# Graph attention on one core: P turned by VectorE in 32x32 blocks and moved through DRAM, K and V projected in bursts, values three tiles behind

## The reference

```
q, k, v = (x @ Wq), (x @ Wk), (x @ Wv)      each reshaped to (8, 2048, 256)
a = q @ k.T / 16 + adj + adj                # per head, 2048 x 2048
a = where(adj == 0, -1e6, a);  a = softmax(a);  a = where(adj == 0, 0, a)
out = layernorm(x + concat_heads(a @ v) @ Wout)
```

## Time and profile before

| | |
|---|---|
| median of three runs | 2095.36 us |
| span of the profiled execution, first to last instruction | 2092.3 us |
| time around that span, against the median of the runs | 3.1 us |
| TensorE busy | 2043.2 us, 98% |
| VectorE busy | 1159.7 us, 55% |
| ScalarE busy | 843.0 us, 40% |
| GpSimd busy | 264.9 us, 13% |
| DMA | 226.42 MB, mean 108 GB/s |

### The profile page before, as it was taken

One profiled execution on the slowest core, in us unless ns is written; L12 is line 12 of the kernel. 1 busy time (PEld: TensorE's weight loads), 2 busy tenths in 40 slices (PEclk: granted clock), 3 DMA queues, 4 the chain that ended last, 5 costly groups with the idle time before them and its releaser, 6 DMA issues.

```text
span 2092.3 us, 36481 instructions
## 1 busy us (share of the span) xinstructions
PE 2043.2 (98%) x12320; PEld 1789.0 (86%) x12320; DVE 1159.7 (55%) x2852; ACT 843.0 (40%) x1364; POOL 264.9 (13%) x207
## 2 busy tenths in 40 slices
PE   7899999999999999999999999999999999999997
PEld 7777788888888888888888888888888888888886
DVE  7788874454545445454555454455445445445555
ACT  4333333443443444334434434443344343343333
POOL 5111111101101101111011011011011111000000
PEclk9999999999999999999999999999999999999999
DMA  6766643333333333233333333333333332323332
GB/s 234 234 205 202 205 141 102 88 89 100 86 101 96 85 96 95 82 101 85 90 103 88 96 94 86 98 99 85 95 100 86 97 96 80 99 81 83 83 87 74
DMA packets 145607, 226.42 MB, mean 108 GB/s; under 512 B 12928, under 2 KB 70272, under 8 KB 143488
## 3 DMA queue, kind: packets, MB, share of 16 engines
q1 hardware_dynamic: 145536, 225.50, 36.9%
HBM read 206.57 MB, written 18.87 MB: 108 GB/s over the span
## 4 chain that ended last, share of the span: by engine, by line
PE 87%; DVE 5%; DMA 2%; issue 2%; ACT 0%; DVEq 0%; SPq 0%
PE bank L153 31%; PE bank L677 19%; PE bank L146 14%; PE bank L676 10%; PE bank L661 10%; DMA m_dram<-m_build 2%; DVE m_build L255 2%; PE bank L673 1%; PE bank L674 1%; DVE t_p L221 1%; DVE zero_mark L243 1%; DVE pt_l L209 0%; DVE k L209 0%; DVE y_acc L519 0%; DVE y_acc L914 0%
## 5 line engine op out<-in xcount | busy, mean ns | idle before, releaser
L153 PE MATMUL bank<-k,q_split 128*128 128x512 f32 x3072 | 840.8, 409 | 3.5 <-DVE k L209 2.5
L677 PE MATMUL bank<-v,pt_h 128*128 128x512 f32 x1856 | 673.5, 395 | 0.0
L153 PEld LDWEIGHTS bank<-k,q_split 128*128 128x128 f32 x3072 | 541.5, 190 | 95.7 <-issue 4.4
L209 DVE TENSOR_TENSOR pt_l<-bank,pt_h 128x512 fp32r<-128x512 f32 x496 | 342.7, 691 | 401.5 <-PE bank L153 392.5
L171 ACT ACTIVATE pt_h<-bank 128x512 fp32r<-128x512 f32 x496 | 296.2, 597 | 615.3 <-PE bank L661 615.2
L676 PE MATMUL bank<-v,pt_l 128*128 128x256 f32 x1856 | 522.5, 282 | 0.0
L677 PEld LDWEIGHTS bank<-v,pt_h 128*128 128x128 f32 x1856 | 348.9, 188 | 69.2
L676 PEld LDWEIGHTS bank<-v,pt_l 128*128 128x128 f32 x1856 | 350.5, 189 | 13.6
L221 DVE CUSTOM_DVE_ANT_0 t_p<-bank,m_sb 128x512 f32<-128x512 f32 x512 | 348.2, 680 | 1.8 <-PE bank L153 1.8
L176 ACT ACTIVATE t_p<-t_p,small 128x2048 f32<-128x2048 f32 x128 | 256.4, 2003 | 164.7 <-DVE small L229 157.5
L661 PE MATMUL bank<-ident,t_p 128*128 128x128 f32 x2048 | 307.6, 273 | 5.8 <-ACT t_p L176 3.7
(11 more groups left out here) (69 smaller groups left out, 1394.7 us busy)
## 6 DMA issues: line engine op xcount, KB each, us to landing
m_sb<-m_dram SPq DMA_DIRECT2D x508, 256.0 KB, 3.2
adj_chunk<-in_adj_dram SPq DMA_DIRECT2D x64, 256.0 KB, 3.0
raw_w_q<-in_L_gnn_Wq_dram SPq DMA_DIRECT2D x63, 256.0 KB, 3.7
raw_w_k<-in_L_gnn_Wk_dram SPq DMA_DIRECT2D x56, 256.0 KB, 3.9
raw_w_v<-in_L_gnn_Wv_dram SPq DMA_DIRECT2D x56, 256.0 KB, 4.1
m_dram<-m_build SPq DMA_DIRECT2D x14, 1024.0 KB, 5.0
raw_x<-in_x_dram SPq DMA_DIRECT2D x8, 256.0 KB, 4.4
place<-in_L_gnn_Wv_dram SPq DMA_DIRECT2D x8, 256.0 KB, 6.4
```

The source lines that it names most:

```text
L153: mm = nc.tensor.matmul(score_bank[b][:], q_split[:, a, k, f * P:(f + 1) * P], k_both[:, kk, k, b * BANK:(b + 1) * BANK], start=(i == 0), ...
L209: ins = nc.vector.tensor_tensor(dst, src, hi.bitcast(F32), ALU.subtract)
L677: mm = nc.tensor.matmul(*hi_v, start=False, stop=(g == BANKS - 1 and j == TPB - 1))
```

## The change

**P's path.** The transposes on TensorE are gone. VectorE turns `t_p` (all 2048 columns, one instruction) in blocks of 32x32 into `blocks`, sorted by the block's place inside its 128 columns (`turn`). SP stores `blocks` to DRAM (`park`, 1 MB, rows of 8 KB), and loads it back in four pieces of 256 KB (`shuffle`), piece i from 32 rows of DRAM to all 128 partitions, so that each 128x128 block lies fully turned in `p_turned`. ScalarE writes the high part (`hi_p`), GpSimd the low part (`lo_p`), each in four pieces a tile. The values of a tile are multiplied three steps after its scores (`LAG = 3`), and P's split and the sum in PSUM have two buffers.

**K and V.** There is one K and one V buffer. All eight K slices of a head are projected in one burst ahead of its tile 0, all eight slices of V (transposed and times Wout) in one burst ahead of tile 3's scores. Weights go through five slots, loaded five ahead. Every projection and every bank of scores takes the next of a ring of six PSUM banks; two more hold the sums. Q stays one slice per two tiles.

**M.** It is loaded whole (1 MB), by ScalarE's queue, into one of two buffers. In head 0 one tile of M is made during the tile before, with two `adj_chunk` buffers, whose loads stand between the loads of P in SP's order. The prologue is gone, and all code is unrolled.

```diff
+LAG = 3
+RING = 6
+SLOTS = 5
+        p_dram = nc.dram_tensor("p_dram", [2, P, N], F32, kind="Internal").ap()
+        m_sb = [sbuf(f"m_sb{i}", [P, N]) for i in range(2)]
+        blocks = [sbuf(f"blocks{i}", [P, N]) for i in range(2)]
+        p_turned = sbuf("p_turned", [P, N])
+        p_split = [sbuf(f"p_split{i}", [P, 2, N], F32R) for i in range(2)]
+        adj_chunk = [y_acc[:, Y_LATE + 2 * i:Y_LATE + 2 * i + 2, :].rearrange("p a d -> p (a d)") for i in range(2)]
...
+                def park(tau):
+                    sp.wait_ge(turned, tau + 1)
+                    if tau >= 2:
+                        for i in range(QUADS):
+                            sp.wait_ge(shuffled[i], 16 * (tau - 1))
+                    sp.dma_start(p_dram[tau % 2], blocks[tau % 2][:]).then_inc(parked, 16)
+
+                def shuffle(tau, i):
+                    if i == 0:
+                        sp.wait_ge(parked, 16 * (tau + 1))
+                    if tau:
+                        sp.wait_ge(p_lo, 4 * (tau - 1) + i + 1)
+                    sp.dma_start(p_turned[:, i * BANK:(i + 1) * BANK],
+                                 p_dram[tau % 2][quad(i), :].rearrange("p (j b) -> j p b", j=QUADS)
+                                 ).then_inc(shuffled[i], 16)
...
+                for tau in range(ALL + 1):
+                    h, t = divmod(tau, TILES)
+                    if h == 0:
+                        store_m(t)
...
+                    if opens:
+                        if h:
+                            load_wout(h)
+                        load_w_behind("k", h, 2)
+                    if sums:
+                        load_w_behind("vt", h, 1)
+                    if tau:
+                        park(tau - 1)
+                    for i in range(QUADS):
+                        if opens:
+                            load_w_behind("k", h, 3 + i)
+                        if sums:
+                            load_w_behind("vt", h, 2 + i)
+                        if tau:
+                            shuffle(tau - 1, i)
+                        if h == 0 and t + 1 < TILES:
+                            load_adj((t + 1) * BANKS + i)
...
+                for tau in range(ALL + LAG):
+                    h, t = divmod(tau, TILES)
+                    if tau < ALL and t == 0:
+                        if h:
+                            wait_emptied(("x", h))
+                        for c in range(C):
+                            project_x(("k", h, c))
+                        project_x(("q", h, 0))
+                    if tau < ALL and t == VALUES_FROM:
+                        pe.wait_ge(wout_lo, h + 1)
+                        for c in range(C + 1):
+                            if c < C:
+                                project_x(("vt", h, c))
+                            if c:
+                                wait_emptied(("vt", h, c - 1))
+                                project(("v", h, c - 1), vt_split[(c - 1) % 2], w_out)
+                    for g in range(BANKS):
+                        if tau < ALL:
+                            scores(tau, g)
+                            if g == 1 and t % 2 == 0 and t <= LAST_Q:
+                                project_x(("q", h, t // 2 + 1))
+                            if g == 1 and t == TURN_X and h + 1 < H:
+                                turn_x(h + 1)
+                        if tau >= LAG:
+                            values(tau - LAG, g)
...
+                def hi_p(tau, i):
+                    if i == 0 and tau >= 2:
+                        act.wait_ge(y_done, tau - 1)
+                    act.wait_ge(shuffled[i], 16 * (tau + 1))
+                    nc.scalar.activation(by_chunk(p_split[tau % 2][:, HI])[:, :, i, :],
+                                         p_turned[:, i * BANK:(i + 1) * BANK].rearrange("p (j b) -> p j b", b=QUAD),
+                                         ACT.Copy).then_inc(p_hi, 1)
...
+                def turn(tau):
+                    if tau >= 2:
+                        dve.wait_ge(parked, 16 * (tau - 1))
+                    dve.wait_ge(exp_done, tau + 1)
+                    nc.vector.transpose(blocks[tau % 2][:].rearrange("p (q j b) -> p j q b", q=QUADS, b=QUAD),
+                                        t_p[:].rearrange("p (j q b) -> p j q b", q=QUADS, b=QUAD)
+                                        ).then_inc(turned, 1)
```

More of the change, by code:

```diff
@@ L80, in graph_attention_layernorm @@
-        before = ExitStack()
[L81 to L85, removed]
+        k_split = sbuf("k_split", [P, 2, KC, N], F32R)
+        v_split = sbuf("v_split", [P, CHUNKS, 2, D], F32R)
+        q_split = [sbuf(f"q_split{i}", [P, 2, KC, R], F32R) for i in range(2)]
+        vt_split = [sbuf(f"vt_split{i}", [P, 2, KC, R], F32R) for i in range(2)]
@@ L122, in graph_attention_layernorm @@
[L122 to L128, removed]
+        ln = sbuf("ln", [P, 144])
@@ L140, in graph_attention_layernorm @@
         TERMS = [(a, b, k) for k in range(KC) for a, b in ((HI, HI), (HI, LO), (LO, HI))]
[L142 to L186, removed]
@@ new lines, in _, with store_out @@
+                assert loaded[0] == len(w_keys)
+                def store_out(first, stop):
+                    for f in range(HALVES):
+                        sp.dma_start(out_tokens[f][:, first:stop], y_tokens[:, f, first:stop]).then_inc(stored, 16)
+                sp.wait_ge(normed, 8)
+                store_out(0, 4)
+                sp.wait_ge(normed, TILES - 2)
+                store_out(4, C - 1)
+                for f in range(HALVES):
+                    sp.wait_ge(normed, TILES - 1 + f)
+                    sp.dma_start(out_tokens[f][:, C - 1], y_tokens[:, f, C - 1]).then_inc(stored, 16)
@@ new lines, in score @@
+                def score(tau, b):
+                    r, t = home["s", tau, b][0], tau % TILES
+                    dve.wait_ge(scores_done, BANKS * tau + b + 1)
+                    if b == 0 and tau >= TILES:
+                        dve.wait_ge(m_loaded[tau % 2], 16 * (tau // 2 - TILES // 2 + 1))
+                    if b == 0 and tau:
+                        dve.wait_ge(turned, tau)
+                    if tau < TILES:
+                        dve.wait_ge(m_chunk, (tau + 1) * BANKS)
+                    nc.vector.tensor_tensor_reduce(out=t_p[:, b * BANK:(b + 1) * BANK], in0=bank[r][:],
+                                                   in1=m_sb[tau % 2][:, b * BANK:(b + 1) * BANK], scale=2.0,
+                                                   scalar=LOWEST, op0=ALU.add, op1=ALU.max,
+                                                   accum_out=maxima[:, t, b:b + 1]).then_inc(emptied[r], 1)
@@ new lines, in denominator @@
+                def denominator(tau):
+                    t = tau % TILES
+                    dve.wait_ge(floor_done, tau + 1)
+                    nc.vector.scalar_tensor_tensor(out=row_sum[:, t:t + 1], in0=floor_exp[:, t:t + 1],
+                                                   scalar=count[:, t:t + 1], in1=row_sum[:, t:t + 1],
+                                                   op0=ALU.mult, op1=ALU.add).then_inc(denom_ready, 1)
+                    dve.wait_ge(denom_ready, tau + 1)
+                    nc.vector.reciprocal(rdenom[:, t:t + 1], row_sum[:, t:t + 1]).then_inc(rdenom_ready, 1)
```

1047 lines of the change are left out of this document (445 added, 602 removed).

## The result

The changed kernel takes 2813.19 us (median of 4 runs, 2807.79 to 2815.39) against 2095.32 us before: a ratio of 1.3429, 95% interval 1.341 to 1.3448. It is 34% slower. The forecast was 2560 us, slower, range 2180 to 2830.

The account below looks back on a forecast made before the run. TensorE, busy 2043.2 of 2092.3 us, was taken to bound the kernel before. Forecast: 7 heads x (16 x 18.2 + 10) = 2109, head 0 400, 27 before the first store, 25 after the last: 2560 us, range 2180 to 2830.

Parts of the forecast that it names:

- The mechanism: Loads of P in every tile: source counts 4 outermost, so four DMA engines carry each, 2.73 us a load.
- The period: Per tile on those four engines: 18.2 us taken, low 16.8, high 19.4; above 16.0 slower than before.
- 10.9, 2.4 and 2.6 us: Parts of one period: P's four loads 10.9 us, the store's share 2.4, one fixed latency 2.6.
- M's and the weights' 3.5: End of each period: M's share 2.4 us and weights 1.1, which may fall into the 2.6 us latency or not.
- its stock of three tiles keeps the DMA engines fed, all but 0 to 10 us a burst: Two bursts a head: TensorE stalls, its stock keeps DMA fed; 0 to 20 us lost a head, 10 taken.
- Head 0: Ring of store, loads of P and adj, last chunk, add_y, transpose: 25.3 us, less with overlap; 16 x 25 = 400 us.
- Start and end: Before the first store 27 us (K burst 13, first load and splits 8, scores and exponential 6); after the last 25.
- The forecast's own high sum: Whole kernel, upper end: 7 x (16 x 19.4 + 20) + 450 + 60 = 2823 us.
- Costs on the engines: Per tile: VectorE 8.4 us with transpose 2.4, ScalarE 7.3 to 9.7, GpSimd 7.2 to 12.4, all beside TensorE's 14.4.
- rival D: VectorE's 32x32 transpose or GpSimd's strided low parts take several times longer and set the period: 2110 us or more; chance 0.04.
- Rival C: TensorE, waiting each tile, gets half clock half the time, its 14.4 us become 21.6: 2874 us; chance 0.05.
- Rival B: The four loads run on all 16 engines, TensorE's 14.4 us a tile rule: 2038 us, faster; chance 0.14.

Follow-up runs that it names:

- 16-engine version: Against the changed kernel, P stored so each load's source is 128 contiguous rows, the store in four transfers: 2159.52 us, ratio to before 1.0313.

## Why the prediction was right, and what it mis-sized

**The mechanism: right.** Four engines carry the loads of P (4 small packets each, and one row of padding switches between 2160 and 2917 us); their period sets the pace of the regular steps; TensorE waits at values for `p_lo`, 293.6 us in 70 waits. A load was taken at 2.73 us on four engines and came 2.5 to 2.6 us behind the one before it, once 3.2. By the rule of the Trainium skill ("DMA: Bandwidth & Descriptors", "Why a DMA increments its semaphore by 16 and not by 1") the loads get four engines, and the trace agrees, with 2048 small packets for 512 loads.

**The period: right, slightly high.** 18.2 us was taken; between bursts it is 17.65, and the 14 regular steps of a head, some of which draw on stock, average (331 - 93) / 14 = 17.0 us. The prediction's 10.9, 2.4 and 2.6 us make 15.9, and the short period of the chain is 15.95; the long one, 19.35, is its high end. So on average 1.1 to 1.75 us of M's and the weights' 3.5 come on top, less than was taken. The long period also has slow issues in it (2.92 us for a load of P, 2.52 for the weights, where others take 0.5). With the weights in ScalarE's queue the long steps were still 18 to 19 us, so these issues are at most a small part.

**The step that failed: "its stock of three tiles keeps the DMA engines fed, all but 0 to 10 us a burst".** A head's two burst steps take 46 + 47 = 93 us; by the prediction's terms 2 x 18.2 + 10 = 46. The 47 us too few, less 17 us too many in the regular steps, are the 30 us by which a head is longer (331 for 301), 6 heads 180 us. The prediction had SP behind TensorE and the weights late, as it is, but let the loads of P run on meanwhile. In the trace from 1120 to 1166 us, a burst of K, TensorE is busy 28.09 of 46 us at a clock of 0.74 and the DMA share is no higher than elsewhere:

```profile
1120.00:1166.00 46.00, 28.09 (x144) 24.74 (x144) 12.37 (x23) 16.21 (x29) 19.58 (x16) 0.74 0.46 146
```

SP's queue (L257 the store of P, L264 its loads) and VectorE's next transpose say why the stock didn't help (start, duration, what):

```profile
1123.67 1.63 SPq L257 DMA_DIRECT2D p_dram<-blocks  x1
...
1134.24 0.54 SPq L264 DMA_DIRECT2D p_turned<-p_dram  x1
...
1147.56 0.54 SPq L264 DMA_DIRECT2D p_turned<-p_dram  x1
...
1163.38 2.31 DVE L608 STREAM_TRANSPOSE blocks<-t_p 128x2048 f32<-128x2048 f32 x1 [0.75 <-ACT t_p L507]
...
1165.72 0.34 SPq L257 DMA_DIRECT2D p_dram<-blocks  x1
```

Between two stores of P 42 us pass, with four loads, one tile, in them; the next tile can only be stored once it is turned, and its scores come behind the burst in TensorE's order. What stock there is lies between the loads and the values: it feeds TensorE, and not the DMA engines.

Weights by another queue took back 18 us of the two steps' 93, and 22 to 26 us per head. Why the rest (75 us in the two steps of that run against 64 on 16 engines) remains was not taken apart further.

**Head 0: right in its ring, short in its sum.** 25.3 us for a period was worked out and 26 us measured, and taking adj out of the ring cut it by 7 us on 16 engines. The sum took 25 x 16 = 400 and left out that head 0 has its burst of V and the next head's K in it too (52.6 and 49.3 us): 458 us.

**Start and end.** The first transpose starts at 46.9 us, for 27 predicted ahead of the first store. The first burst of K ends at 28.4 us for 21, and the scores and the exponential of the first tile take 18 us for 6, with the making of the next tile's M between the scores in VectorE's order and ScalarE idle for 9.85 us until a weight of V comes. From the last transpose's start to the end it is 53 us for 25, at a clock of 0.69; these 53 hold the last tile's store and loads, which the prediction counted as head 7's last period. Together 48 us. Head 7 has 15 distances, none with a burst of K: 270 us, 31 less than 301. 180 + 58 + 48 - 31 = 255 us is the distance from 2560 to 2814.

**Luck in the range.** 2813 us lies 17 us inside the upper end. The forecast's own high sum, 2823 us, has heads of 330 us by regular steps of 19.4 and 20 us for two bursts; the measured heads of 331 us have 17.0 and 93 - 2 x 17.0 = 59 us. A size too small by 39 us a head and one too large by 38 cancel in it.

**A term put at nothing.** TensorE also waits for x of the next head, 104.8 us in eight waits of up to 15.5 us. What it costs in this kernel is not shown: the step with the wait takes 26 to 27 us, but the one after it 11.1, and two regular steps take 35 to 36 together.

**Costs on the engines: right.** The transpose took 2.31 us (2.4 taken), hi_p 626 ns, so 2.5 us for four (2.4 taken), lo_p 1284 ns on its strided shape (1.29): rival D has nothing for it. An issue of SP mostly took 0.5 us, not 0.4.

**Rival C: half right.** The clock fell to 0.854, in the stretches above to 0.57, 0.74 and 0.69. In the regular steps it didn't set the time: 2.6 us more of TensorE's work in each left them as long. Its part in the burst steps, the start and the end is open.

**Rival B, had it been so:** 2038 us was worked out, 2160 measured. Its TensorE term holds (heads of 244 us, 235 by its sum), its head 0 was 404 for 355 us, its start and end 87 for 35 (first transpose at 47.7 us, 39.0 us from the last to the end); and it had no wait for x, of which there were 48 us (eight, the row below, over the whole kernel of 16 engines: idle time of TensorE's L364 and what ended it).

```profile
PE bank L364 <- DMA raw_x<-in_x_dram: 48.0, 8, 10.4
```

## What to carry to other kernels

Before a DMA goes into a loop's period, compare the outermost counts of its two sides: a rearrangement that puts a small count first on the source leaves most engines idle, and a layout in DRAM that makes the read contiguous cost three issues more a tile here. A mean DMA share under one half is no sign of room, as the 0.48 here with four engines full; divide the small packets by the transfers to see how many engines each one had. When a transfer queue serves a fast consumer and a slow producer in one written order, look at which of them it is late for: here three moves of issues (adj ahead of P, weights to the other queue, x a step later) turned the 3% loss of the 16-engine version into a gain of 4.8%.

## What the runs showed of the hardware that was not expected

A 32x32 transpose of 128x2048 fp32 with scattered blocks took 2.309 to 2.310 us on VectorE in every kernel, no more than the 2.4 us of a plain pass carried on from the earlier trace rows. With four engines loaded, a store that uses all 16 lands 11.6 us after its issue instead of 5.0. GpSimd's subtraction cost 1.28 to 1.30 us for 128x512, contiguous or in runs of 32, with VectorE busy beside it.
